# A two-layer graph network on one core: row loads moved from SyncE's queue to ScalarE's, and two units' column sums to VectorE

## Chip, core and metric

One NeuronCore of a Trainium2 chip runs the whole program. The metric is the device time of one execution in microseconds (us); lower is better.

## What is computed

`x` is 2048 x 512, `adj` is 2048 x 2048, both float32; the weight is 512 x 512. Cut to what matters:

```python
h = relu(layernorm(x))
q = round(min(h / a, 1) * 15)                      # 4-bit activations
w = round(|clip(wnorm / b, -1, 1)| * 7) * sign     # 3-bit weights
s = round(min(relu(q @ w * scale) / a2, 1) * 15)
x1 = x + adj @ s * scale                           # layer 0
h = relu(layernorm(x1))
A = (adj + adj.T) * 0.5 + I
dinv = where(rowsum(A) > 0, rowsum(A) ** -0.5, 0)
out = x1 + (1e-8 * ones) @ (dinv * A * dinv) @ h   # layer 1 of the source
```

(The last layer's coefficient matrix is in the call the adjacency itself: the function is called as `_L1_gnn(h, adj, adj)`, so the result is `x1 + adj @ ((dinv * A * dinv) @ h)`.) Both row sums and column sums of `adj` are needed for `dinv`.

## The kernel before

`adj` is worked on in 32 units: unit u is half a row block, 128 rows by 1024 columns of float32, 512 KB. Each unit has to lie in the buffer `at` transposed and split in two float16 halves ("hi", scaled by 256 and rounded, and "lo", the rest). TensorE needs them as the stationary side in layer 0 and again in the last product. A unit gets there in one of two ways:

- **Turned** units (`TURNED`): TensorE transposes the float32 unit into PSUM (`turn`, L1081), ScalarE writes hi out of PSUM (`hi_turned`, L520), VectorE writes lo (`lo_turned`, L758) and sums the columns (L745); ScalarE makes the row sum (`row_sum`, L484).
- **Moved** units (`MOVED`, 21 of them): ScalarE writes hi of the untransposed rows into a staging place (`hi_rows`, L509, which makes the row sum as well), VectorE writes lo (`lo_rows`, L763), and the SyncE queue (SP) issues two DMA transposes, hi and lo, from the staging place to `at` (`move`, L339). There are three staging places: `hi_rows` of the k-th moved unit waits until the move of the (k-3)-th has landed. The even moved units (10, 12, 14, 18, 20, 22, 26) need column sums of their own: `sum_blocks` (L496) on ScalarE, eight blocks a unit, in two calls of four. Odd moved units are added up by GpSimd into `acc` (L461, 15 additions in order), which TensorE turns once ("acc").

Layer 0 (`layer0`, L1102) has 16 rounds, one for each row block r: 32 products of 128 x 128 by 128 x 512 into one PSUM bank, with the turns of that round in between (`TURNS`). `layer0(r)` waits for `x1_ready` of round r-2, for unit 2r before its first product and for unit 2r+1 before j = 8. VectorE's `x1_tile` (L884 to L887) writes round r's result into `feat` and takes its statistics. After layer 0 come the sweeps with the symmetrized matrix (L1167, from about 159 us) and the last product (L1204, L1220).

The order on every queue is written out by hand. Per round r, VectorE does `x1_tile(r-1)`, what the turned unit needs, `lo_rows` of `MOVES[r]`, and in some rounds a late column sum (`column_sum_late`, L751: hi and lo of one unit out of `at`, in one reduction; rounds 3 and 5 for units 0 and 2) or a piece of the next stage (`sum_unit`, L930 to L935: unit 0 in round 8, unit 1 in round 10; `sum_lo`, L940). ScalarE does `hi_turned`, `hi_rows`, `row_sum` and the block sums of `SUMS_OF` in turn. SyncE does the moves, and behind them the row loads (`rows`, L314): the list `LOADS` says behind which move unit w is loaded. From unit 20 on a load overwrites an earlier unit's place, so `rows_again` first waits in `free_slot` (L318 to L329) for the readers of that unit: `acc_done` (GpSimd), `lo_ready` (VectorE), or `turned` and `rs_done`. Places for input: units 0 to 3 and 20 to 31 share the four slots of `a_in`; units 4 to 19 lie in parts of `at` that are filled later.

Turning unit 30 (round 13, L1081) waits for the lo half of unit 28 (L758); `hi_turned(28)` (L523 to L526) waits for the moves of units 26 and 27, since unit 28's place in `at` is used for staging. Before layer 0's round 14, TensorE waits for all parts of `sum_blocks`.

Of the kernel before, what the change touches and what calls it, by code (L numbers as in the profile page):

```python
# [6 lines left out]
P = 128  # L7
# [4 lines left out]
W = N // 2  # L12
B = W // P
UNITS = 2 * T
# [13 lines left out]
SUMMED = EVEN  # L28
# [6 lines left out]
def gnn_kernel(nc, x, adj, adj_scale, weight, wgt_alpha, act_alpha, act_alpha2, out):  # L35
# [5 lines left out]
    with ctx:  # L41
# [236 lines left out]
        for u in EVEN:  # L278
# [13 lines left out]
        SUMS_OF = {5: [[(10, FIRST)], [], [(10, LAST)]], 7: [[(12, FIRST)], [(12, LAST)], []],  # L292
                   8: [[(14, FIRST)], [(14, LAST)], []], 9: [[(18, FIRST)], [(18, LAST)], []],
                   10: [[], [], [(20, FIRST)]], 11: [[], [(20, LAST)], [(22, FIRST)]],
                   12: [[], [], [(22, LAST), (26, FIRST)]], 13: [[], [], [(26, LAST)]]}
        PARTS = sum(len(place) for places in SUMS_OF.values() for place in places)

# [9 lines left out]

        @block.sync
        def _(sp):
            def load_x(n):  # L310
                sp.dma_start(feat3[:, 2 * n:2 * n + 2, :], x_tiles[:, 2 * n:2 * n + 2, :]).then_inc(x_in[n], 16)

            def rows(u):
                sp.dma_start(unit_in(u), adj[(u // 2) * P:(u // 2 + 1) * P, (u % 2) * W:(u % 2 + 1) * W])\  # L314
                  .then_inc(arr_sem(u), 16)

            def rows_again(u):
                free_slot(before(u))  # L318
                rows(u)

            def free_slot(u):

                if u in ADDED:
                    sp.wait_ge(acc_done, ADDED.index(u) + 1)
                if u in MOVED:
                    sp.wait_ge(lo_ready, MOVED.index(u) + 1)
                else:
                    sp.wait_ge(turned, turn_no(u) + 1)
                    sp.wait_ge(rs_done, TURNED.index(u) + 1)  # L329

            def move(u):
                for lo, ready in ((0, hi_ready), (1, lo_ready)):
                    sp.wait_ge(ready, MOVED.index(u) + 1)
                    if u == 29:
                        wait_moved(sp, MOVED[-3])
                        wait_moved(sp, MOVED[-2])
                    elif u >= 12:
                        free_slot(waited_in(u)[lo])
                    sp.dma_start_transpose(at_half(u // 2, lo, u % 2).rearrange("p (b i) -> p b i", i=P), stage(u, lo))\  # L339
                      .then_inc(at_moved[stage_no(u)][lo], 16)  # L340
# [14 lines left out]
            rows(0)  # L355
            rows(1)
            for n in range(2, T // 2):
                load_x(n)
            for u in range(2, 12):
                rows(u)  # L360
# [3 lines left out]
            rows(12)  # L364
            rows(13)
# [3 lines left out]
            rows(14)  # L369
            rows(15)  # L370
            move(7)
            LOADS = {9: [16], 10: [17], 11: [18], 12: [19], 13: [20], 14: [21], 15: [22], 17: [23], 20: [24], 21: [25], 22: [26],
                     23: [27], 25: [29, 28], 26: [30], 27: [31]}
            for r in range(1, 12):
                for u in MOVES[r]:
                    move(u)
                    for w in LOADS.get(u, []):
                        if w < AHEAD:
                            rows(w)
                        else:  # L380
                            rows_again(w)
            for v in range(2, 6):
                free_slot(UNITS - 6 + v)
                sums(v)
# [79 lines left out]
        def _(act):  # L464
# [14 lines left out]
            def row_sum(u):  # L479
                act.wait_ge(arr_sem(u), arrivals(u))  # L480
                act.wait_ge(turned, turn_no(u) + 1)
                if u in ADDED:
                    act.wait_ge(acc_done, ADDED.index(u) + 1)
                nc.scalar.activation(unit_in(u), unit_in(u), ACT.Copy, accum_out=rowsum[:, u:u + 1]).then_inc(rs_done, 1)  # L484

# [136 lines left out]
            for r in range(1, 14):  # L622
                moves = MOVES.get(r, [])
                ahead, between, behind = SUMS_OF.get(r, [[], [], []])
                for u in TURNS[r][:1]:
                    turn_hi(u)
                for u, blocks in ahead:
                    sum_blocks(u, blocks)
                for u in moves[:1]:
                    hi_rows(u)  # L630
                for u in TURNS[r][:1]:
                    sum_rows(u)
                for u in TURNS[r][1:]:
                    turn_hi(u)
                    sum_rows(u)
                for u, blocks in between:
                    sum_blocks(u, blocks)
                for u in moves[1:]:
                    hi_rows(u)
                for u, blocks in behind:  # L640
                    sum_blocks(u, blocks)
                if r == 9:
                    sum_hi(0)
                if r == 11:
                    sum_hi(1)
# [22 lines left out]
        def _(dve):  # L668
# [278 lines left out]
            for r in range(1, 14):  # L947
# [11 lines left out]
                if r - 3 in LATE_SUMS:  # L959
                    column_sum_late(r - 3)  # L960
                if r == 8:
                    sum_unit(0)
# [8 lines left out]
            link(nc.vector.memset(pause[:, :], 0.0))  # L971
            link(nc.vector.tensor_scalar(colp[:, a:b], colp[:, a:b], 1.0 / SA, None, ALU.mult))
# [276 lines left out]
```

## Time and profile before

| | us |
|---|---|
| median of 3 runs (493.93 to 495.35) | 495.15 |
| the profiled execution's own time | 496.49 |
| its span | 494.7 |
| TensorE busy | 478.1 (97%) |
| VectorE, ScalarE, GpSimd busy | 268.5, 154.1, 46.6 |

The profile is of one execution. Its span runs from the first to the last instruction; 1.8 us of its own time lie around it. A busy TensorE is shown by modelled ends, so short idle times between matmuls read a little smaller than the distance of the starts makes them. A queue ("SPq") is an engine's sequencer: the instructions that issue DMAs stand there.

### The profile page before, as it was taken

Reading aid. Unit: us, or ns where it says so; the run is one execution under the profiler, and the core shown is the slowest. Engines: PE = TensorE matmul, PEld = TensorE weight load, DVE = VectorE, ACT = ScalarE, POOL = GpSimd, SP = SyncE. Lnnn points to the kernel's source line nnn. Section 1 sums busy time; section 2 is a strip of 40 time slices with the busy share of each in tenths; the row PEclk is TensorE's granted clock in tenths of the full one; section 3 lists DMA queues with packets and bytes.
Section 4 is the critical chain, followed back from the end, with each engine's and each line's share of the span. In section 5 each row is a group of like instructions: output and inputs, shape, how many; then the busy total and the mean of one; then the engine's idle time right before and its main releaser. Section 6 shows DMA issues by size and latency. Waiting matters only on the chain.

```text
span 494.7 us, 6414 instructions
## 1 busy us (share of the span) xinstructions
PE 478.1 (97%) x2358; PEld 232.0 (47%) x2358; DVE 268.5 (54%) x360; ACT 154.1 (31%) x300; POOL 46.6 (9%) x54
## 2 busy tenths in 40 slices
PE   1899999999999999999999999999999999999997
PEld 1755544444454444444444444444444444444446
DVE  4966996779999688876997767340100001000010
ACT  1787833767562435344521121140000000000000
POOL 2320963213200000000000000000000000000000
PEclk9999999999999999999999999999999999999999
DMA  8986999999986242332232321045010000100001
GB/s 286 401 333 161 233 193 231 225 220 229 233 241 249 65 135 98 95 117 85 85 122 91 113 99 42 0 168 193 23 42 21 21 21 21 42 21 21 21 23 43
DMA packets 63180, 62.66 MB, mean 127 GB/s; under 512 B 46136, under 2 KB 46392, under 8 KB 63160
## 3 DMA queue, kind: packets, MB, share of 16 engines
q1 hardware_dynamic: 63152, 62.40, 44.3%
q8 instruction: 11, 0.18, 0.2%
q14 instruction: 9, 0.07, 0.0%
q10 hardware_dynamic: 8, 0.00, 0.0%
HBM read 42.99 MB, written 8.39 MB: 104 GB/s over the span
## 4 chain that ended last, share of the span: by engine, by line
PE 84%; DVE 8%; DMA 4%; SPq 2%; ACT 1%; issue 1%; POOL 0%; ACTq 0%
PE ps_a L1204 31%; PE ps_p L1102 13%; PE ps_p L1167 7%; PE ps_a L1167 7%; PE ps_b L1167 7%; PE ps_m L1167 4%; PE ps_h L1167 4%; DMA feat<-in_x 2%; PE ps_b L1053 1%; PE ps_m L1102 1%; PE ps_h L1102 1%; DVE at L763 1%; DVE small L944 1%; PE ps_b L1220 1%; PE ps_a L1220 1%; PE ps_a L1053 1%
## 5 line engine op out<-in xcount | busy, mean ns | idle before, releaser
L1102 PE MATMUL ps_p<-small,at 128*128 128x512 f16 x448 | 99.2, 379 | 0.4 <-DVE feat L884 0.4
L1022 DVE SCALAR_TENSOR_TENSOR feat<-ps_a,feat 128x512 f32<-128x512 f32 (+1 forms) x16 | 10.8, 675 | 148.7 <-PE ps_a L1204 144.2
L1204 PE MATMUL ps_a<-small,at 128*128 128x512 f16 x360 | 80.2, 379 | 0.0
L1204 PE MATMUL ps_a<-a_in,at 128*128 128x512 f16 x360 | 80.2, 379 | 0.0
L1102 PEld LDWEIGHTS ps_p<-small,at 128*128 128x128 f16 x448 | 43.7, 98 | 50.8 <-DVE feat L884 0.7
L584 ACT ACTIVATE split<-a_in 128x1024 f16<-128x1024 f32 x30 | 31.7, 1057 | 101.8 <-PE ps_p L1167 90.0
L940 DVE TENSOR_TENSOR split<-a_in,split 128x1024 f16<-128x1024 f32 x30 | 36.7, 1224 | 34.0 <-ACT split L584 34.0
L1204 PEld LDWEIGHTS ps_a<-small,at 128*128 (+1 forms) x360 | 35.2, 98 | 42.5
L1204 PEld LDWEIGHTS ps_a<-a_in,at 128*128 (+1 forms) x360 | 35.2, 98 | 42.5
L1167 PE MATMUL ps_p<-feat,split 128*128 (+1 forms) x180 | 43.9, 379 | 0.5 <-DVE small L944 0.5
L1167 PE MATMUL ps_a<-feat,split 128*128 (+1 forms) x180 | 43.8, 379 | 0.0
L1167 PE MATMUL ps_b<-feat,split 128*128 (+1 forms) x180 | 43.8, 379 | 0.0
L931 DVE TENSOR_TENSOR a_in<-a_in,at 128x1024 f32<-128x1024 f32 x30 | 36.7, 1225 | 1.0
L930 DVE SCALAR_TENSOR_TENSOR a_in<-a_in,at 128x1024 f32<-128x1024 f32 x30 | 36.5, 1217 | 0.0
L1167 PEld LDWEIGHTS ps_p<-feat,split 128*128 128x128 f16 x180 | 17.5, 98 | 22.0 <-DVE small L944 1.0
L1167 PEld LDWEIGHTS ps_a<-feat,split 128*128 128x128 f16 x180 | 17.6, 98 | 21.4 <-issue 0.5
L1167 PEld LDWEIGHTS ps_b<-feat,split 128*128 128x128 f16 x180 | 17.6, 98 | 21.2
L1167 PE MATMUL ps_m<-feat,split 128*128 (+1 forms) x90 | 24.3, 379 | 0.0
L1167 PE MATMUL ps_h<-feat,split 128*128 (+1 forms) x90 | 24.3, 379 | 0.0
L461 POOL TENSOR_TENSOR at<-at 128x1024 f32<-128x1024 f32 x8 | 21.4, 2673 | 12.6 <-PE ps_p L1102 11.8
L763 DVE SCALAR_TENSOR_TENSOR at<-at 128x1024 f16<-128x1024 f32 x12 | 18.9, 1600 | 0.0
L461 POOL TENSOR_TENSOR at<-at,a_in 128x1024 f32<-128x1024 f32 x6 | 15.2, 2526 | 28.5 <-DMA a_in<-in_adj 18.4
(182 smaller groups left out, 436.0 us busy)
## 6 DMA issues: line engine op xcount, KB each, us to landing
a_in<-in_adj SPq DMA_DIRECT2D x46, 512.0 KB, 3.9
at<-in_adj SPq DMA_DIRECT2D x16, 512.0 KB, 8.9
out<-feat SPq DMA_DIRECT2D x31, 256.0 KB, 4.3
feat<-in_x SPq DMA_DIRECT2D x8, 512.0 KB, 11.6
feat<-out SPq DMA_DIRECT2D x4, 1024.0 KB, 9.3
at<-in_L_gnn_weight SPq DMA_DIRECT2D x2, 512.0 KB, 4.0
at<-at SPq DMA_TRANSPOSE x42, 4.7
split<-in_adj SPq DMA_DIRECT2D x1, 512.0 KB, 15.7
```

Of the source, the lines that this page charges most:

```text
L461: nc.gpsimd.tensor_tensor(acc, acc, unit_in(u), ALU.add).then_inc(acc_done, 1)
L584: nc.scalar.activation(part(v % 2, 0), sum_in(v), ACT.Copy).then_inc(shi, 1)
L763: nc.vector.scalar_tensor_tensor(stage(u, 1), unit_in(u), SA, stage(u, 0), ALU.mult, ALU.subtract)\
L930: link(nc.vector.scalar_tensor_tensor(u3, u3, SA, at_across(h, 0, j), ALU.mult, ALU.add))
L931: last = nc.vector.tensor_tensor(u3, u3, at_across(h, 1, j), ALU.add)
L940: nc.vector.tensor_tensor(part(v % 2, 1), sum_in(v), part(v % 2, 0), ALU.subtract).then_inc(slo, 1)
L1022: nc.vector.scalar_tensor_tensor(out, products, 1.0 / (SA * SZ), out, ALU.mult, ALU.add).then_inc(y_out, 1)
L1053: last = nc.tensor.matmul(sup_banks(m)[:, t * D:(t + 1) * D], hT[m % 2][:, (t * KD + k) * P:(t * KD + k + 1) * P], w_int[:, k * D:(k + 1) ...
L1102: last = nc.tensor.matmul(l0_bank(r), at_block(r, lo, j), small[:, j * D:(j + 1) * D], start=(j == 0 and lo == 0), stop=(j == T - 1 and lo ...
L1167: last = nc.tensor.matmul(BANK[t], part(k, lo)[:, t * P:(t + 1) * P], g_part(j, g_lo), start=(first and lo + g_lo == 0), stop=False)
L1204: last = nc.tensor.matmul(BANK[n], at_block(t, lo, j), z_part(j, z_lo), start=(j == 0 and lo + z_lo == 0), stop=(j == T - 1 and lo == 1))
L1220: last = nc.tensor.matmul(BANK[1 + h][:, 0:DH], at_block(T - 1, lo, j), z_part(j, z_lo)[:, h * DH:(h + 1) * DH], start=(j == 0 and lo + z_ ...
```

## The change

1. The loads of units 16 to 31 are issued by ScalarE, on its own DMA queue, behind `hi_rows(u)` or `sum_rows(u)` of a unit u (`load_behind`), from unit 20 on after the same `free_slot` waits, now on ScalarE. SyncE issues the moves alone in rounds 1 to 11. The list `LOADS` changes a little: unit 24 goes behind 21 instead of 20, 25 behind 22, 26 behind 23, 28 behind 24, 27 behind 25, 29 behind 26, 30 behind 27, 31 behind 29.
2. The column sums of units 10 and 14 are no longer made in `sum_blocks` on ScalarE (16 blocks less), but by `column_sum_late` on VectorE in rounds 5 and 7, and 16 sums are scaled once more behind layer 0's rounds. Units 18, 20, 22 and 26 get their block sums a round or so earlier than before, and none is left in round 13.

```diff
-SUMMED = EVEN
+SUMMED_LATE = (10, 14)
...
-        SUMS_OF = {5: [[(10, FIRST)], [], [(10, LAST)]], 7: [[(12, FIRST)], [(12, LAST)], []],
-                   8: [[(14, FIRST)], [(14, LAST)], []], 9: [[(18, FIRST)], [(18, LAST)], []],
-                   10: [[], [], [(20, FIRST)]], 11: [[], [(20, LAST)], [(22, FIRST)]],
-                   12: [[], [], [(22, LAST), (26, FIRST)]], 13: [[], [], [(26, LAST)]]}
+        SUMS_OF = {7: [[(12, FIRST)], [(12, LAST)], []], 8: [[(18, FIRST)], [(18, LAST)], []],
+                   9: [[(20, FIRST)], [(20, LAST)], []], 10: [[(22, FIRST)], [], [(22, LAST)]],
+                   12: [[], [], [(26, FIRST), (26, LAST)]]}
...
+        LOADS = {9: [16], 10: [17], 11: [18], 12: [19], 13: [20], 14: [21], 15: [22], 17: [23], 21: [24], 22: [25],
+                 23: [26], 24: [28], 25: [27], 26: [29], 27: [30], 29: [31]}
...
+        def rows(engine, u):
+            engine.dma_start(unit_in(u), adj[(u // 2) * P:(u // 2 + 1) * P, (u % 2) * W:(u % 2 + 1) * W])\
+                  .then_inc(arr_sem(u), 16)
+
+        def free_slot(engine, u):
...
         @block.sync
...
-            LOADS = {9: [16], 10: [17], 11: [18], 12: [19], 13: [20], 14: [21], 15: [22], 17: [23], 20: [24], 21: [25], 22: [26],
-                     23: [27], 25: [29, 28], 26: [30], 27: [31]}
             for r in range(1, 12):
                 for u in MOVES[r]:
                     move(u)
-                    for w in LOADS.get(u, []):
-                        if w < AHEAD:
-                            rows(w)
-                        else:
-                            rows_again(w)
...
         @block.scalar
...
+            def load_behind(u):
+                for w in LOADS.get(u, []):
+                    if w >= AHEAD:
+                        free_slot(act, before(w))
+                    rows(act, w)
...
                 for u in moves[:1]:
                     hi_rows(u)
+                    load_behind(u)
                 for u in TURNS[r][:1]:
                     sum_rows(u)
+                    load_behind(u)
...
                 for u in moves[1:]:
                     hi_rows(u)
+                    load_behind(u)
...
         @block.vector
...
                 if r - 3 in LATE_SUMS:
                     column_sum_late(r - 3)
+                for k, u in enumerate(SUMMED_LATE):
+                    if r == (5, 7)[k]:
+                        wait_moved(dve, u)
+                        column_sum_late(u)
...
             link(nc.vector.memset(pause[:, :], 0.0))
+            late_sums = colp[:, :].rearrange("p (u b) -> p u b", b=B)[:, SUMMED_LATE[0]:SUMMED_LATE[-1] + 1:4, :]
+            nc.vector.tensor_scalar(late_sums, late_sums, 1.0 / SA, None, ALU.mult)
```

## Rows read from the trace of the kernel before

**Rows 1.** Waits of TensorE, 24 to 160 us: us in total, times, longest

```profile
PE ps_a L1081 <- DVE at L758: 0.9, 1, 0.9
```

**Rows 2.** Chain that ended last, in order of time: start, us, what (rates)

```profile
139.71 0.87 PE ps_b L1081 x8
...
145.77 6.91 PE ps_h L1102 x32
```

**Rows 3.** Timeline 110 to 135 and 135 to 160 us, TensorE: start, us, instruction, [idle before <-releaser]

```profile
126.63 1.04 PE L1081 MATMUL ps_a<-ident,a_in 128*128 128x128 f32 x8
...
128.11 1.90 PE L1102 MATMUL ps_p<-small,at 128*128 128x512 f16 x8 [0.44 <-DVE feat L884]
...
136.92 1.06 PE L1081 MATMUL ps_a<-ident,a_in 128*128 128x128 f32 x8 [0.86 <-DVE at L758]
```

**Rows 4.** Timeline 110 to 135 us: VectorE, ScalarE and GpSimd

```profile
110.88 1.06 ACT L509 ACTIVATE at<-a_in 128x1024 f16<-128x1024 f32 x1 [4.16 <-DMA a_in<-in_adj]
...
112.06 2.30 DVE L763 SCALAR_TENSOR_TENSOR at<-a_in,at 128x1024 f16<-128x1024 f32 x1 [2.88 <-ACT at L509]
...
115.42 0.74 DVE L884 SCALAR_TENSOR_TENSOR feat<-ps_p,cst,feat 128x512 f32<-128x512 f32 x1
...
119.78 2.91 POOL L461 TENSOR_TENSOR at<-at,a_in 128x1024 f32<-128x1024 f32 x1 [6.49 <-DMA a_in<-in_adj]
...
120.39 3.38 DVE L930 SCALAR_TENSOR_TENSOR tmp<-tmp,at 128x1024 f32<-128x1024 f32 x1
...
127.31 0.74 DVE L884 SCALAR_TENSOR_TENSOR feat<-ps_p,cst,feat 128x512 f32<-128x512 f32 x1
...
128.91 2.33 DVE L763 SCALAR_TENSOR_TENSOR at<-a_in,at 128x1024 f16<-128x1024 f32 x2
...
133.37 1.02 ACT L520 ACTIVATE at<-ps_a 128x1024 f16<-128x1024 f32 x1 [4.88 <-DMA at<-at]
```

**Rows 5.** Timeline of SyncE's queue, 100 to 107.2 and 119 to 134.5 us

```profile
99.26 2.65 SPq L339 DMA_TRANSPOSE at<-at  x2
101.96 0.58 SPq L314 DMA_DIRECT2D a_in<-in_adj  x1
...
106.51 0.53 SPq L314 DMA_DIRECT2D a_in<-in_adj  x1
...
119.60 1.88 SPq L314 DMA_DIRECT2D a_in<-in_adj  x2
```

**Rows 6.** ScalarE's block sums L496 and VectorE's late sums L751

```profile
L496 ACT ACTIVATE ps_h<-at x4: 364/367/368, 71.9 to 76.8; 128x256 f32<-128x256 f16 x4
...
L751 DVE TENSOR_REDUCE colp<-at x2: 2272/2272/2272, 68.3 to 80.2; 128x8 f32<-128x2048 f16 x2
```

**Rows 7.** Row loads L314: issued 57 to 132 us, and the two of 119.9 to 122

```profile
L314 SPq DMA_DIRECT2D a_in<-in_adj x12: 521/532/1253, 77.9 to 131.5; - x12
...
DMA to landing us min/median/max: 4.2/4.6/5.9
...
DMA to landing us min/median/max: 4.8/5.2/5.6
```

**Rows 8.** The page's groups: busy us, mean ns of one, idle before

```profile
L930 DVE SCALAR_TENSOR_TENSOR a_in<-a_in,at 128x1024 f32<-128x1024 f32 x30 | 36.5, 1217 | 0.0
```

**Rows 9.** Moves issued 92 to 102.5, then 102.5 to 120 us: time to landing

```profile
DMA to landing us min/median/max: 3.1/3.3/5.4
...
DMA to landing us min/median/max: 4.2/5.0/6.1
```

**Rows 10.** Stretches: us; busy PE, PEld, DVE, ACT, POOL; clock, DMA share, GB/s

```profile
92.00:102.00 10.00, 10.00 (x48) 4.51 (x46) 7.59 (x9) 6.94 (x26) 4.24 (x2) 1.00 1.02 202
102.00:120.00 18.00, 18.00 (x89) 8.70 (x88) 14.40 (x16) 11.89 (x37) 2.58 (x2) 1.00 1.09 234
```

**Rows 11.** Timeline of VectorE, 144 to 145 and 156 to 161 us

```profile
144.45 0.18 DVE L972 TENSOR_SCALAR colp<-colp 128x24 f32<-128x24 f32 x1
...
159.62 0.75 DVE L884 SCALAR_TENSOR_TENSOR feat<-ps_m,cst,feat 128x512 f32<-128x512 f32 x1 [0.75 <-PE ps_m L1102]
```

More of the change, by code:

```diff
@@ L306, in arrivals @@
             return 16 if u < AHEAD else 16 * ((u - AHEAD) // RING + 2)
+        def rows(engine, u):
+            engine.dma_start(unit_in(u), adj[(u // 2) * P:(u // 2 + 1) * P, (u % 2) * W:(u % 2 + 1) * W])\
+                  .then_inc(arr_sem(u), 16)
+        def free_slot(engine, u):
+            if u in ADDED:
+                engine.wait_ge(acc_done, ADDED.index(u) + 1)
+            if u in MOVED:
+                engine.wait_ge(lo_ready, MOVED.index(u) + 1)
+            else:
+                engine.wait_ge(turned, turn_no(u) + 1)
+                engine.wait_ge(rs_done, TURNED.index(u) + 1)
         @block.sync
@@ L311, in load_x @@
                 sp.dma_start(feat3[:, 2 * n:2 * n + 2, :], x_tiles[:, 2 * n:2 * n + 2, :]).then_inc(x_in[n], 16)
[L313 to L326, printed above, removed]
-                else:
-                    sp.wait_ge(turned, turn_no(u) + 1)
-                    sp.wait_ge(rs_done, TURNED.index(u) + 1)
             def move(u):
@@ L337, in move @@
                     elif u >= 12:
-                        free_slot(waited_in(u)[lo])
+                        free_slot(sp, waited_in(u)[lo])
                     sp.dma_start_transpose(at_half(u // 2, lo, u % 2).rearrange("p (b i) -> p b i", i=P), stage(u, lo))\
@@ L354, in _ @@
                 load_x(n)
-            rows(0)
-            rows(1)
+            rows(sp, 0)
+            rows(sp, 1)
             for n in range(2, T // 2):
@@ L359, in _ @@
             for u in range(2, 12):
-                rows(u)
+                rows(sp, u)
             sums(0)
@@ L363, in _ @@
             sp.wait_ge(hT_ps, T // 2)
-            rows(12)
-            rows(13)
+            rows(sp, 12)
+            rows(sp, 13)
             move(3)
@@ L368, in _ @@
             sp.wait_ge(sq_ready, T // 2)
-            rows(14)
-            rows(15)
+            rows(sp, 14)
+            rows(sp, 15)
             move(7)
-            LOADS = {9: [16], 10: [17], 11: [18], 12: [19], 13: [20], 14: [21], 15: [22], 17: [23], 20: [24], 21: [25], 22: [26],
-                     23: [27], 25: [29, 28], 26: [30], 27: [31]}
             for r in range(1, 12):
@@ L376, in _ @@
                     move(u)
-                    for w in LOADS.get(u, []):
-                        if w < AHEAD:
-                            rows(w)
-                        else:
-                            rows_again(w)
             for v in range(2, 6):
-                free_slot(UNITS - 6 + v)
+                free_slot(sp, UNITS - 6 + v)
                 sums(v)
```

## Prediction

> **What bounds the kernel now.** I read the table first: TensorE is busy 97% of the span, so the question is where the rest is and whether this change reaches it. The waits of TensorE between 24 and 160 us, where the change works, leave little: the longest is 0.9 us before a turn, for VectorE's L758 [rows 1]. The timeline places them. The turn of unit 28 starts at 126.63 and has 8 matmuls; a turn takes 0.87 us [rows 2], so it ends at 127.50, and the products of round 12 start at 128.11, after VectorE's `x1_tile(10)` [rows 3]: 0.61 us lost. Round 12 has 32 products at 6.91 us and the turn "acc" of 0.87 [rows 2], so from 128.11 it ends at 135.89; unit 30's turn starts at 136.92 [rows 3]: 1.03 us lost. Together **1.64 us**. Everywhere else in this stretch the starts of the matmuls follow each other without a hole, so this is the most that the change can bring in layer 0.
>
> Who is late? Going back from 136.92: VectorE's lo of unit 28, ScalarE's hi of it at 133.37 after 4.88 us of idling for a DMA transpose [rows 4], the lo move of unit 27. That move could only be issued once `lo_rows(27)` was through, the first of the two at 128.91 [rows 4]. `lo_rows(27)` stood behind `x1_tile(10)` at 127.31, this behind `sum_unit(1)` from 120.39, this behind `x1_tile(9)` at 115.42, and the head of this unbroken VectorE chain is `lo_rows(25)` at 112.06, which had waited 2.88 us for ScalarE, and ScalarE 4.16 us for unit 25 to arrive [rows 4]. Both holes of TensorE thus come from one late load: unit 25 was asked for at 106.51, behind unit 21's moves [rows 5].
>
> **Loads to ScalarE.** On SyncE's queue a load and two transposes took 4.55 us (101.96 to 106.51), two transposes without a load 2.65 [rows 5]. Of the loads, unit 25's counts. Now ScalarE issues it behind `hi_rows(22)`, once `lo_rows(21)` is done. That was done before unit 21's second transpose went out, and the first went out right behind the load at 101.96, so some time between 102 and 104. The late sum of unit 14 may push it 2.27 us on [rows 6], at most. So the load goes out between 102 and 104.5 (with ends this near I take 103.5), and with 4.2 to 5.9 us to landing [rows 7] it is there at about 108.3 instead of 110.9. `lo_rows(25)` starts at about 109.5 instead of 112.06, and TensorE's round 9 ends at 126.63 - 2 x 6.91 - 0.87 = 111.94, so `x1_tile(9)` starts at about 112.5 instead of 115.42: **the chain is 2 to 3 us earlier**.
>
> Behind it may lie more. `sum_unit(1)`'s first step took 3.38 us [rows 4] where the mean is 1.22 [rows 8], beside GpSimd's addition of unit 27 at 119.78, which itself had waited 6.49 us for its load [rows 4]. With units 27 and 29 loaded earlier, these additions come before or behind `sum_unit(1)`: zero to 2 us more. I take 3 us for `x1_tile(10)`: 124.3 instead of 127.31. The first hole needs 0.61 and is gone. `lo_rows(27)` comes as much earlier. Its move had 3.1 us to landing; beside a load such moves had a median of 5.0 [rows 9], and unit 31's load now goes out at the same moment, since both wait for `lo_rows(27)`. So of 3 us some 1.9 may be given back: hi of unit 28 starts 1.1 to 3 us earlier, or more by GpSimd's part. The second hole needs 1.64 (its own 1.03 and the 0.61 by which TensorE now comes earlier). I take the hole as closed, since 1.1 is the corner and not the middle, and keep 0 to 0.5 us left over for the range.
>
> **What ScalarE pays.** 16 loads at 0.53 us [rows 7] are 8.5 us; 16 block sums less, at 0.37 us and the reading of each sum, about 0.4, are 6.4 us. Net 2 us over some 80 us in which it is busy about two thirds (11.89 of 18 us [rows 10]); idling covers it. What it pays in order is more delicate: its waits in `free_slot` now hold everything behind them, `hi_rows` and `hi_turned` among them. Followed for the tightest: the turn of unit 24 ends at 126.63 - 2 x 6.91 = 112.8 as before; then hi of it (1.02), four block sums of unit 22 (1.6), `hi_rows(26)` (1.15), load 29 (0.55), the row sum (1.15), so load 28 goes out at about 118.4, lands by 122.6 to 124.3, and is needed at 126.63. Before, it was the second of the two loads from 119.60 [rows 5], at most 5.6 us to landing [rows 7], and there some 0.8 us ahead of its turn.
>
> **What SyncE gains.** Its moves no longer stand behind loads and their waits. Nothing that TensorE waits for hangs on it but units 26 and 27 above. The loads of the next stage wait on `rs_done` of units 28 to 31 as before and come with the turns.
>
> **Late sums on VectorE.** Two at 2.27 us [rows 6]. Unit 10's, in round 5, and unit 14's, in round 7, lie before the head of the chain; VectorE idled 10 - 7.59 = 2.4 us between 92 and 102 and 3.6 us between 102 and 120 [rows 10], and the second of these covers what the first doesn't. `x1_tile` has a round (6.91) of slack. Both moves have long landed. If that cover were gone, a sum costs up to 2.27 us of the chain's 3. The new scaling of 16 sums is like the one of 24, 0.18 us, in a chain that ends before VectorE idles 0.75 us for TensorE [rows 11]: nothing. No block sum is left in round 13, so round 14 doesn't wait for one now that TensorE comes earlier.
>
> **Sum.** -0.61 - 1.03 = -1.64 us; costs 0. The profiled execution's 496.49 becomes 494.85. It stands 1.34 above the median, so against that: 495.15 - 1.64 = **493.5**. Behind layer 0 everything keeps its distance to TensorE and shifts with it.
>
> **A rule that speaks against it.** Between 92 and 102 us, with a single load, the engines' share of busy time is 1.02, and 1.09 with loads between 102 and 120 [rows 10]: they look full either way. The Trainium skill (DMA: Bandwidth & Descriptors, "Issuing engines are not separate DMA queues") says that DMAs of different issuing engines run on the same 16 DMA engines and interleave, so only the issue time is saved. By it the transposes would lose what the loads win, and the time would come out at about 494.5. The sum above doesn't rest on more bandwidth, but on asking for unit 25 earlier.
>
> **Rivals.**
> 1. *The engines are the limit (0.17).* For it: the shares just named, and 4.55 against 2.65 us, which is a load's time whichever queue it is in. Unit 25 still comes earlier, but each move lands 1.9 us later, the first hole closes and the second stays: 495.15 - 0.61 = 494.5.
> 2. *VectorE is no earlier (0.08).* The late sum of unit 14 moves `lo_rows(21)`, `lo_rows(23)` and with them the `free_slot` waits of loads 25 and 27, so that they go out when they did. Against it: it takes 2.27, the load wins 2 to 4.5. No change, 495.15.
> 3. *ScalarE is blocked and unit 28 comes late (0.07); slower.* Place: the turn of unit 28 at 126.63. Each us by which its load lands later costs one; since both holes are then swallowed, it decides from 126.63 + 1.64 = 128.3, that is 4 to 5.7 us later than worked out. Each of loads 25 to 29 waits on ScalarE for VectorE or GpSimd, and such waits add up through `hi_rows` and its transposes, which themselves delay `lo_rows`. At 6 to 8 us of such delay unit 28 is there at about 130.3: +2.0, 497.2.
> 4. *The loads stay tied to the old order (0.03):* ScalarE, in order, reaches them no sooner than SyncE did. 495.15.
>
> **Numbers.** The forecast, both holes closed, has 0.65; 0.17, 0.08, 0.07 and 0.03 for the rivals. About 0.3% (1.5 us) is what a measurement of this kernel can tell from no change. The forecast's 1.64 lies just over it; the runs shown differ by 1.4, so a median may stray by some 0.5, and I give it 0.72 to be seen as faster, 0.28 as the same. Faster: 0.65 x 0.72 + 0.17 x 0.1 = 0.48, with the rest 0.01 for a chain that I missed: 0.49. Slower: 0.06. Same: 0.45. Range: 492.5 (1.64, the stray of a median and the 0.5 by which two medians differ) to 495.8 (rivals 1, 2, 4 and the stray); rival 3 is left out.
>
> **What would show it.** Right: the load of unit 25 issued by ScalarE before 104.5 and `lo_rows(25)` before 110.5; `x1_tile(10)` before 126; no idle time before the products of round 12, nor before the turn of unit 30; round 14 in the chain at 144.1 rather than 145.77 [rows 2]; SyncE's moves pairwise in about 2.7 us. Rival 1: moves landing 5 us and more after issue while loads run, a hole before unit 30's turn. Rival 3: TensorE idle before unit 28's turn for a DMA. The prediction is wrong if TensorE has a new wait anywhere between 50 and 126 us, or if the sweeps no longer follow without a hole.

## The result, and the profile after

The changed kernel takes **508.48 us** (median of 6 runs, 500.19 to 515.92), the kernel before 495.24 beside it (493.93 to 495.35). The ratio is 1.0164, 95% interval 1.0128 to 1.0199: slower, where 493.5 was forecast. The ratios in this text compare only runs within 1.5% of a kernel's fastest (here 500.19, 502.64 and 506.61), so they can be smaller than the quotient of the medians. The profiled execution is one of the longer ones: 513.68 us, span 511.8, against 496.49 and 494.7. The sizes read from it below are therefore those of a long execution; a shorter one of nearly the same kernel, 508.82 us, follows among the experiments and shows the same kinds of waits.

The waits of TensorE in the whole span, of after (the waits for `scal_row` and `wstat` lie outside layer 0 and were there before):

```profile
PE ps_p L1109 <- DMA at<-at: 6.0, 2, 4.9
...
PE ps_a L1088 <- DMA a_in<-in_adj: 5.4, 1, 5.4
...
PE ps_a L1088 <- DVE at L759: 2.1, 1, 2.1
```

Where there had been one wait of 0.9 us [rows 1] there are now four, three of them for DMAs. The timeline of TensorE places them (layer 0's products are L1109 now, turns L1088):

```profile
82.94 1.04 PE L1088 MATMUL ps_a<-ident,at 128*128 128x128 f32 x8
85.10 7.07 PE L1109 MATMUL ps_p<-small,at 128*128 128x512 f16 x32 [1.12 <-DMA at<-at]
97.08 23.18 PE L1109 MATMUL ps_p<-small,at 128*128 128x512 f16 x96 [4.91 <-DMA at<-at]
120.09 1.04 PE L1088 MATMUL ps_b<-ident,a_in 128*128 128x128 f32 x8
120.96 13.98 PE L1109 MATMUL ps_p<-small,at 128*128 128x512 f16 x64
140.33 1.97 PE L1088 MATMUL ps_a<-ident,a_in 128*128 128x128 f32 x8 [5.39 <-DMA a_in<-in_adj]
142.09 3.62 PE L1109 MATMUL ps_p<-small,at 128*128 128x512 f16 x8
145.50 1.35 PE L1088 MATMUL ps_b<-ident,at 128*128 128x128 f32 x8
146.69 5.34 PE L1109 MATMUL ps_p<-small,at 128*128 128x512 f16 x24
154.08 1.06 PE L1088 MATMUL ps_a<-ident,a_in 128*128 128x128 f32 x8 [2.06 <-DVE at L759]
```

With 0.216 us a product and 0.87 a turn [rows 2], the distances of the starts give the holes: 1.29 before 85.10, 5.07 before 97.08 (11.98 less 32 products), 5.55 before 140.33 (19.37 less 64 products), 2.21 before 154.08: **14.12 us**. The two holes before 97.08 and 140.33 cost a second time. Behind 97.08 the 96 products take 23.01 us instead of 20.74; behind 140.33 the turn takes 1.76 instead of 0.87, the 8 products 3.41 instead of 1.73, the turn "acc" 1.19 instead of 0.87: 5.16 us in all. The stretches (us; busy PE, PEld, DVE, ACT, POOL; granted clock, DMA share, GB/s) show why, and something else:

```profile
68.00:72.00 4.00, 4.00 (x20) 1.83 (x19) 3.58 (x4) 0.00 (x0) 2.35 (x1) 1.00 0.80 70
...
92.00:96.00 4.00, 0.17 (x1) 0.00 (x0) 3.93 (x6) 0.00 (x0) 2.34 (x1) 0.87 1.24 95
96.00:100.00 4.00, 2.92 (x7) 1.04 (x8) 2.61 (x3) 2.95 (x11) 0.00 (x0) 0.50 1.10 211
...
140.00:144.00 4.00, 3.67 (x13) 2.46 (x14) 2.01 (x4) 0.00 (x0) 0.00 (x0) 0.50 1.50 124
```

After TensorE had idled some 5 us, its granted clock is 0.50, which is the level of 1.2 GHz. So 14.12 - 1.64 (the holes of before) + 5.16 = 17.6 us; the spans differ by 17.1, and TensorE had started layer 0's turns 0.5 us earlier than before. The loss of this execution is accounted for.

The other thing is in the last two columns: at 68 to 72 us the DMA engines moved 70 GB/s, at 92 to 96 us 95 GB/s, with a busy share of 0.80 and 1.24. The kernel before moved 202 GB/s between 92 and 102 us [rows 10], and at 68 to 72 us, from its trace:

```profile
68.00:72.00 4.00, 4.00 (x20) 1.77 (x19) 3.93 (x5) 1.16 (x3) 2.07 (x1) 1.00 0.87 201
```

So the DMA engines are about as busy as before, or more so, and move a third to a half of the data. The transfers show it. ScalarE's loads (L312) issued between 56 and 150 us, the one issued at 62.24 alone, then the moves (L338) issued in 56 to 150, and those issued at 132 to 134 us alone:

```profile
DMA to landing us min/median/max: 4.4/6.5/11.8
...
DMA to landing us min/median/max: 11.2/11.2/11.2
...
DMA to landing us min/median/max: 3.2/7.3/16.0
...
DMA to landing us min/median/max: 12.4/14.2/16.0
```

Before, loads took 4.2 to 5.9 [rows 7], moves at most 6.1 [rows 9]. Not every load is slow. In the order of issue, start and time to landing of ScalarE's loads are, from the trace:

```text
55.6+4.6  60.7+4.9  62.2+11.2  73.6+4.4  75.4+9.4  85.2+4.6  86.7+10.2  105.3+4.5
110.2+4.6  112.2+9.3  121.8+4.5  124.9+6.5  128.5+11.8  130.2+11.4  137.8+11.8
```

In this trace a load that goes out while ScalarE's previous one has not landed, with moves in flight, takes 9 to 12 us (once 6.5); one that goes out with no other load of ScalarE's in flight takes 4.4 to 4.9. Moves in flight with a slow load are stretched too: the slowest beside each took 10.4 to 16.0 us. ScalarE then waits for staging places: the wait of `hi_rows` (L507) for moves grew from 13.3 us in 5 to

```profile
  DMA at<-at: 37.8, 9
```

and the chain between 60 and 160 us is no longer TensorE's. Its shares by line were 44.5% for layer 0's products in `ps_p` and 3.1% for `DMA at<-at`; now:

```profile
by line: DMA at<-at 55.3%; SPq L338 14.5%; DVE at L764 9.7%; issue 5.1%; PE ps_p L1109 4.1%; ACT at L507 3.6%; DVE feat L885 2.0%; DVE st L887 1.7%; ACT ps_m L494 1.6%; ACT ps_h L494 1.4%; DVE split L932 1.2%; DVE colp L746 1.2%; DVE split 
```

### The profile page after: what moved, and what is told of

Read it like the earlier page. It is cut to its first block, busy times and chain, and to the rows that moved or that the text cites. A ratio compares the mean times of both kernels' runs of the same rounds, so it can differ in the third digit from the quotient of the medians.

```text
span 511.8 us, 6383 instructions
## 1 busy us (share of the span) xinstructions
PE 484.4 (95%) x2358; PEld 234.8 (46%) x2358; DVE 270.4 (53%) x363; ACT 147.8 (29%) x268; POOL 46.5 (9%) x54
## 3 DMA queue, kind: packets, MB, share of 16 engines
q10 hardware_dynamic: 2312, 8.39, 7.9%
HBM read 42.99 MB, written 8.39 MB: 100 GB/s over the span
## 4 chain that ended last, share of the span: by engine, by line
PE 70%; DMA 13%; DVE 8%; SPq 4%; ACT 3%; issue 2%; POOL 0%; ACTq 0%
PE ps_a L1211 30%; DMA at<-at 11%; PE ps_p L1174 7%; PE ps_a L1174 7%; PE ps_b L1174 7%; PE ps_m L1174 4%; PE ps_h L1174 4%; SPq L338 3%; DVE at L764 2%; DMA feat<-in_x 2%; PE ps_p L1109 2%; PE ps_b L1060 1%; PE ps_m L1109 1%; PE ps_h L1109 1%; DVE small L945 1%
## 5 line engine op out<-in xcount | busy, mean ns | idle before, releaser
L1109 PE MATMUL ps_p<-small,at 128*128 128x512 f16 x448 | 103.3, 390 | 6.0 <-DMA at<-at 6.0
L1109 PEld LDWEIGHTS ps_p<-small,at 128*128 128x128 f16 x448 | 44.6, 100 | 59.3 <-issue 11.4
L1174 PEld LDWEIGHTS ps_a<-feat,split 128*128 128x128 f16 x180 | 17.6, 98 | 21.4 <-issue 0.5
L1174 PEld LDWEIGHTS ps_b<-feat,split 128*128 128x128 f16 x180 | 17.6, 98 | 21.2
L764 DVE SCALAR_TENSOR_TENSOR at<-at 128x1024 f16<-128x1024 f32 x12 | 19.0, 1594 | 10.4 <-ACT at L507 10.4
L453 POOL TENSOR_TENSOR at<-at 128x1024 f32<-128x1024 f32 x8 | 21.3, 2667 | 12.6 <-PE ps_p L1109 11.8
L507 ACT ACTIVATE at<-at 128x1024 f16<-128x1024 f32 x12 | 12.6, 1052 | 29.7 <-DMA at<-at 29.7
```

What stands on the lines that cost most here:

```text
L453: nc.gpsimd.tensor_tensor(acc, acc, unit_in(u), ALU.add).then_inc(acc_done, 1)
L507: nc.scalar.activation(stage(u, 0), unit_in(u), ACT.Copy, scale=SA, accum_out=rowsum[:, u:u + 1])\
L764: nc.vector.scalar_tensor_tensor(stage(u, 1), unit_in(u), SA, stage(u, 0), ALU.mult, ALU.subtract)\
L1109: last = nc.tensor.matmul(l0_bank(r), at_block(r, lo, j), small[:, j * D:(j + 1) * D], start=(j == 0 and lo == 0), stop=(j == T - 1 and lo ...
L1174: last = nc.tensor.matmul(BANK[t], part(k, lo)[:, t * P:(t + 1) * P], g_part(j, g_lo), start=(first and lo + g_lo == 0), stop=False)
```

## The experiments

Two theories stand in what follows. Theory A: row loads and DMA transposes that run beside each other from two queues slow each other, whatever their order. Theory E, formed when the third kernel missed: what is slow is a second load of ScalarE's queue, issued while its first is in flight beside transposes. Other explanations stand as rivals in the expectations.

**Each half alone.** The first kernel is the kernel before with the second part of the change (`SUMMED_LATE`, the new `SUMS_OF`, the late sums and their scaling), the second is the changed kernel without it.

```diff
-SUMMED = EVEN
+SUMMED_LATE = (10, 14)
```

> The second half of the change alone: the column sums of units 10 and 14 late on VectorE and the new list of block sums; all loads stay on SyncE's queue in their old order. Theory A (row loads on one queue and DMA transposes on another hinder each other in the 16 DMA engines): no loss, 494 to 496. Rival B (the late sums and the new order of ScalarE's work hold up hi_rows and lo_rows, and the moves with them): most of the loss is here, 500 to 508.

494.7 us (10 runs, 494.03 to 495.85), ratio 1.0003 [0.9989, 1.0016]. Both old holes are still there, in its timeline of TensorE:

```profile
127.47 1.90 PE L1107 MATMUL ps_p<-small,at 128*128 128x512 f16 x8 [0.66 <-DVE feat L883]
...
136.29 1.06 PE L1086 MATMUL ps_a<-ident,a_in 128*128 128x128 f32 x8 [0.87 <-DVE at L757]
```

> The first half alone: the loads of units 16 to 31 issued by ScalarE, sums as before. Theory A: the whole loss, 500 to 512, with TensorE waiting for moves or loads that take 9 us and more to land. Rival B: 494 to 497.

506.78 us (504.06 to 513.79), ratio 1.0198 [1.0177, 1.0219], in theory A's range. In the profiled execution (508.82 us) TensorE waits 8.1 us for moves, and the load at 60.6 us takes 12.6 to land. The loads alone make the loss; by themselves the late sums do nothing. Overlap is not always as dear, though: a load that went out here 2.1 us behind the one before, at 113.4 us, landed in 6.3.

**SyncE's moves wait for the loads.** In the changed kernel, `move(u)` first waits until the loads behind unit u have landed.

```diff
+                for w in LOADS.get(u, []):
+                    sp.wait_ge(arr_sem(w), arrivals(w))
```

> The changed kernel, but SyncE holds the moves of a unit back until the load that ScalarE issued behind the same unit has landed, so that loads and transposes overlap much less; every other queue and order is as in the changed kernel. Theory A: most of the loss comes back, 495 to 500, and loads land in under 6 us. Rival C (ScalarE is blocked in free_slot and everything behind it is late): more waiting only adds, 508 to 520.

510.22 us (508.53 to 512.75), ratio 1.0326 [1.0294, 1.0358]: theory A missed, and the number lies in rival C's range. The wait doesn't part what I meant it to. Moves already in flight stay beside the loads, and ScalarE issues its second load meanwhile: 60.1 and 61.7 us, 74.2 and 75.9, 86.7 and 88.3. The first of each pair lands in 4.4 to 4.5 us, the second in 12.1, 10.7 and 10.6. The pair, not the mixture, is what the slow ones have in common. It isn't enough by itself: five later loads of this execution, from 112 to 131 us, also went out with one of ScalarE's still in flight and landed in 4.5 to 6.3 us.

**Transfers alone, in long runs.** A kernel of nothing but transfers:

```diff
+            for k in range(TR):
+                sp.dma_start_transpose(dst(k), src(k)).then_inc(tr_in[k], 16)
...
+            for k in range(LD):
+                act.dma_start(rows_act[:, k * W:(k + 1) * W], adj_rows(k)).then_inc(act_in[k], 16)
```

> The two kinds of transfer by themselves, in six phases one after the other; nothing of the network is computed, the output is x. Phases: 12 transposes on SyncE (as many and as large as 6 moved units); 6 row loads on SyncE; both on SyncE, a load and two transposes in turn; both at once, transposes on SyncE and loads on ScalarE; 6 loads on each queue; transposes on SyncE and loads on ScalarE, one load in flight at a time. From the traces: 16 us, 8 to 12, and 27 (6 x 4.55) for the first three. Theory A: the fourth and sixth take 35 us or more, while the fifth, without transposes, takes 16 to 20. Rival D (the engines only share their time between the queues): the fourth takes as long as the third or less, 20 to 28.

The same 12 transposes and 6 loads, on one queue in turn and on two:

```profile
33.05:61.14 28.09, 0.00 (x0) 0.00 (x0) 1.00 1.04 224
61.59:87.66 26.07, 0.00 (x0) 0.00 (x0) 1.00 0.98 241
```

The expected loss isn't there: two queues are 2 us faster. Theory A, that mixing alone is slow, falls. Single transfers are stretched here as well, a load to 10.0 us and a transpose to 12.1, but the total isn't. With one load in flight at a time (the sixth phase) the same transfers take 27.6 us, so where nothing collapses that wait costs a little.

**One load of ScalarE in flight.** The changed kernel, where ScalarE waits for its previous load before it issues the next:

```diff
+            loaded = []
...
                 for w in LOADS.get(u, []):
+                    if loaded:
+                        act.wait_ge(arr_sem(loaded[-1]), arrivals(loaded[-1]))
+                    loaded.append(w)
```

> The changed kernel, but ScalarE issues no load before its previous one has landed. Theory E (what is slow is a second load queued on ScalarE's queue while transposes are on SyncE's; a lone load beside transposes landed in 4.4 to 4.9 us in the changed kernel, a second one in 9 to 12): loads land in under 6 us, 495 to 500, though ScalarE waits more. Theory A in its plain form (any overlap of load and transposes is slow in this kernel): 503 to 515. Rival C (blocked ScalarE): also over 503, but with loads that land fast.

**494.19 us** (10 runs, 493.06 to 495.26), ratio 0.9977 [0.9966, 0.9988], the fastest kernel of this study and a little below theory E's range of 495 to 500. ScalarE waits for loads in addition and the kernel is faster, so blocking ScalarE (rival C) isn't what made the loss. Its loads and moves issued between 56 and 150 us land in:

```profile
DMA to landing us min/median/max: 4.0/4.4/6.5
...
DMA to landing us min/median/max: 3.2/5.0/7.9
```

and TensorE between 112 and 140 us:

```profile
112.99 13.98 PE L1114 MATMUL ps_p<-small,at 128*128 128x512 f16 x64
126.80 1.04 PE L1093 MATMUL ps_a<-ident,a_in 128*128 128x128 f32 x8
127.67 1.89 PE L1114 MATMUL ps_p<-small,at 128*128 128x512 f16 x8
...
130.27 5.34 PE L1114 MATMUL ps_p<-small,at 128*128 128x512 f16 x24
135.70 1.06 PE L1093 MATMUL ps_a<-ident,a_in 128*128 128x128 f32 x8
```

Round 12 follows its turn at once, unit 30's turn comes 0.25 us behind the products where it had been 1.03 [rows 3].

**The same transfers in the network kernel's places, beside busy engines.** Transfers beside work that computes nothing of the network:

```diff
+            for k in range(12):
+                sp.dma_start_transpose(dst(k), src(k)).then_inc(tr_in[k], 16)
+            done(sp, 4)
```

> The transfers by themselves once more, now in the network kernel's own places in SBUF; the network is not computed, the output is x. Six phases: both queues at once (12 transposes on SyncE, 6 loads on ScalarE) with idle engines; three groups of 4 transposes beside 2 loads 1.2 us apart, idle engines; both queues at once beside TensorE's matmuls; the same beside VectorE and GpSimd at work; the same beside all three; one queue in turn beside all three. The earlier run of the same transfers in other places took 26 us on two queues and 28 us on one, so mixing alone isn't slow. If the places matter, the first phase takes 35 us or more; if two queued loads do, the second does (over 12 us a group); if an engine's accesses matter, the phase beside it. If all take 24 to 30, something else of the kernel is needed.

Two queues beside TensorE, beside VectorE and GpSimd, beside all three, and one queue beside all three:

```profile
79.87:107.50 27.63, 27.27 (x120) 12.07 (x120) 0.00 (x0) 0.00 (x0) 0.00 (x0) 1.00 1.04 228
107.95:134.28 26.33, 0.00 (x0) 0.00 (x0) 25.82 (x8) 0.00 (x0) 25.47 (x9) 0.55 0.97 240
134.73:161.56 26.83, 26.51 (x116) 11.77 (x117) 26.55 (x9) 0.00 (x0) 26.11 (x9) 0.94 1.00 235
162.00:190.59 28.59, 26.50 (x123) 11.86 (x121) 28.18 (x10) 0.00 (x0) 27.79 (x10) 1.00 1.03 221
```

Busy engines make it no slower than idle ones did (30.4 us in this kernel, where the first transpose took 15 us to land, 26.07 in the one before), so they are no part of it. Of three short groups (four transposes, two loads) one took 12.35 us, with a second load of 8.6; the order in time seemed to matter, which was an impression and not yet shown.

**An earlier load on one queue.** The kernel before, where loads 24 to 27 and 29 to 31 go out between a unit's hi and lo move:

```diff
+                    if lo:
+                        for w in EARLY.get(u, []):
+                            rows_again(w)
```

> The kernel before, all on SyncE's queue, with the loads of units 24 to 27 and 29 to 31 one step earlier: between the hi and the lo move of the unit behind which they stood (28 stays). The prediction's own reasoning without a second queue: unit 25 arrives some 2.6 us earlier, VectorE's chain starts earlier, both holes of TensorE close, -1.6 us, 493.2. Rival: the moves are pushed back as far as the loads win, no change.

498.59 us (497.06 to 498.92), ratio 1.0062 [1.0042, 1.0081]: missed by both, and slower. The first hole is closed (0.06 us left), the second has grown to 2.75. The lo moves go out behind a load and its waits, and unit 30's turn waits longer, with a half-speed turn behind it:

```profile
137.47 1.79 PE L1086 MATMUL ps_a<-ident,a_in 128*128 128x128 f32 x8 [2.59 <-DVE at L763]
```

**Groups of transfers.** Kind f of the kernel, on ScalarE (`spend(1)` is one activation of 1.06 us):

```diff
+                if kind == "f":
+                    spend(3)
+                    load_f(0)
+                    spend(1)
+                    load_f(1)
```

> Transfers alone, 30 groups with nothing else at work; of the network nothing is computed and the output is x. Each group holds 4 transposes of a move's size on SyncE's queue (6 in kind f), and both queues wait for all of it before the next group. Kinds, 5 of each: a) one load on ScalarE's queue; b) two loads some 1.3 us apart; c) two loads back to back; d) the second load only when the first has landed; e) everything on SyncE's queue, load, two transposes, load, two transposes; f) two loads 1.3 us apart, begun some 4 us behind the first of six transposes. Theory E (a second load in flight on ScalarE's queue beside transposes is what stretches all that is in flight): a load lands in 4 to 5 us in a, d and e, the second load takes 8 to 12 us in b, c and f, and groups b and c are 2 us or more longer than e. Rival (the slow loads need something else of the network kernel, since transfers alone did not show them so far): the second load of b, c and f stays below 7 us and b, c are within 1 us of e.

The five groups of each kind, a to f in order (us; busy DVE, ACT, POOL; clock, DMA share, GB/s):

```profile
11.56:55.56 44.00, 0.00 (x0) 0.00 (x0) 0.00 (x0) 1.00 0.85 179
55.56:107.73 52.17, 0.00 (x0) 6.56 (x6) 0.00 (x0) 1.00 0.92 201
107.73:159.25 51.52, 0.00 (x0) 0.00 (x0) 0.00 (x0) 1.00 0.91 204
159.25:212.34 53.09, 0.00 (x0) 0.00 (x0) 0.00 (x0) 1.00 0.90 198
212.34:265.44 53.10, 0.00 (x0) 0.00 (x0) 0.00 (x0) 1.00 0.90 198
265.44:356.03 90.59, 0.00 (x0) 21.12 (x20) 0.00 (x0) 1.00 1.01 145
```

b and c miss theory E's numbers: as long as e, second loads of 4.8 to 8.8 and 5.5 to 7.0 us. f meets them, every time: second loads of 9.3 to 12.8 us, transposes up to 13.7, at 145 GB/s. So two loads beside transposes are not enough. In f there are six transposes, and the first load comes in when the third of them has been issued and two are in flight; in the changed kernel, too, two or three moves were in flight when each slow load went out. Which of the two differences from b, the later start or the larger number, counts is not parted here.

**Dose and share.** The kernel with one load in flight, first with the column sums as before (the second half of the change undone), then with the wait for the loads up to unit 23 alone:

```diff
-                    if loaded:
+                    if loaded and w < 24:
```

> The loads on ScalarE's queue with one in flight at a time, and the column sums of units 10 and 14 on ScalarE as in the kernel before. If the late column sums have no share in the gain of the changed kernel with one load in flight (494.19), this gives 494.0 to 494.4, as the kernel with the sums alone (ratio 1.0003) suggests. If ScalarE's 16 more block sums delay hi_rows or the loads behind them, 494.7 to 496.

497.9 us (11 runs, 495.64 to 499.21), ratio 1.0053 [1.0034, 1.0072]: missed, and slower than before. Its loads are quick (3.9 to 5.7 us). But ScalarE, which now waits for loads, still has units 22 and 26's sums to make in rounds 12 and 13, and `split` (L588) comes late for VectorE, last at 131.67 us after a wait of 3.22, ahead of the work that unit 30's turn waits for. ScalarE's and VectorE's waits in 94 to 140 us:

```profile
ACT ps_h L500 <- DMA a_in<-in_adj: 8.4, 4, 3.2
...
DVE split L947 <- ACT split L588: 5.8, 2, 3.2
```

```profile
136.89 1.91 PE L1088 MATMUL ps_a<-ident,a_in 128*128 128x128 f32 x8 [2.65 <-DVE at L765]
```

Unit 30's turn comes late and, behind 2.65 us of idle, takes 1.70 us by the starts instead of 0.87. Worth nothing alone, the second half of the change (the late sums together with the new list of block sums, which this run undoes as one) is worth 3.7 us here (497.9 against 494.19).

> The changed kernel where only the loads up to unit 23 wait for ScalarE's previous load; those of 24 to 31 go out as in the changed kernel. Theory E: TensorE's waits before 100 us (1.3 and 5.2 us in the changed kernel) are gone, the one of some 5.7 us before unit 30's turn is still there with a stretch at half clock behind it, and the time is 498 to 506. If the late waits are only a consequence of the early ones (the order of the work shifted by them), they go too: 494 to 495.

498.37 us (10 runs, 494.34 to 512.85), ratio 1.0047 [1.002, 1.0074], just inside theory E's range. The early waits are gone. (The text above says "unit 30's turn" for the wait of some 5.7 us; by the order of the turns it is unit 28's.) The profiled execution is a short one, 495.62: its late loads overlap and take up to 8.0 us, unit 28's 7.1, and TensorE waits 0.3 for it and 1.0 before unit 30's turn. There is no collapse in it, though six of its late loads went out with another of ScalarE's in flight and with two or three moves. The times spread from 494.34 to 499.76 in eight runs, with 506.05 and 512.85 in the other two, where the kernel with all loads in turn spreads over 2.2 us. That the late waits are the reason for the spread is likely but not shown, since none of the long executions was profiled.

**Six transposes, and what comes on top.**

```diff
+                    if kind == "k" and k >= 2:
+                        sp.wait_ge(tr_in[k - 2], 16 * t[k - 2])
+                    if kind == "l" and k in (2, 3):
+                        load(k - 2)
```

> Transfers alone again, 30 groups of six transposes of a move's size on SyncE's queue, nothing of the network computed, the output is x; both queues wait for a whole group before the next. 5 groups of each kind, one after the other: g) six transposes alone; h) one load on ScalarE's queue 3.4 us behind the first transpose; i) two loads from there, the second issued when the first has landed; j) two loads 1.5 us apart, as in kind f of the groups before (14.7 to 19.9 us a group there); k) as j, but SyncE issues a transpose only when the last but one has landed, so that two are in flight; l) everything on SyncE's queue, the loads behind the second and the third transpose. Theory E (two loads of ScalarE's queue in flight beside a queue of transposes are what collapses): g takes 8 to 9.5 us, h 10 to 11.5, i and l 12.5 to 14, j 15 to 20 as before, and the slow loads (over 8 us) are in j alone. Rival (any load that comes in while five transposes are queued collapses, whether alone or not): h and i are slow too, 12 us or more for h and 16 or more for i, with loads over 8 us. Kind k tells whether the depth of the transposes' queue has a part: 12.5 to 14.5 us with loads under 7 us if it has, 15 or more if the two loads do it by themselves.

Kinds g to l, five groups each:

```profile
11.57:62.03 50.46, 0.00 (x0) 0.00 (x0) 0.00 (x0) 1.00 0.82 156
62.03:125.07 63.04, 0.00 (x0) 17.12 (x16) 0.00 (x0) 1.00 0.93 167
125.07:195.84 70.77, 0.00 (x0) 15.84 (x15) 0.00 (x0) 1.00 0.91 185
195.84:288.06 92.22, 0.00 (x0) 21.12 (x20) 0.00 (x0) 1.00 1.01 142
288.06:384.44 96.38, 0.00 (x0) 21.12 (x20) 0.00 (x0) 1.00 0.93 136
384.44:450.69 66.25, 0.00 (x0) 0.00 (x0) 0.00 (x0) 1.00 0.91 198
```

ScalarE's loads in i, then in j, and SyncE's in l:

```profile
DMA to landing us min/median/max: 4.2/4.8/6.0
...
DMA to landing us min/median/max: 5.4/9.7/12.3
...
DMA to landing us min/median/max: 4.4/5.1/6.2
```

A fifth of each stretch is a group: 10.1 us for transposes alone, 12.6 with one load, 14.2 with two in turn, **18.4** with two in flight, 13.3 on one queue. The same bytes take 4 us longer when the second load doesn't wait for the first. That is theory E's order, not all of its numbers: g is above its 9.5 us, h above its 11.5 and i just above its 14. One load alone is a little slow too (5.4 to 6.7 us) and h reaches the rival's 12, but i stays below the rival's 16, and no load of h or i is over 8 us. In j every second load takes 11.3 to 12.3 us. Kind k was the surprise: only two transposes in flight, and 19.3 us, with second loads of 10.4 to 11.4. So a long row of transposes in flight isn't needed; ScalarE's second load is. How much of k's 19.3 us is its own waiting stays open, as it has no group without loads, and in j no more than four transposes are in flight either: issuing one took up to 7.3 us there, 1.3 in g.

**The new list, one queue.** The changed kernel with all loads back behind the moves on SyncE:

```diff
-                    load_behind(u)
...
                     move(u)
+                    for w in LOADS.get(u, []):
+                        if w >= AHEAD:
+                            free_slot(sp, before(w))
+                        rows(sp, w)
```

> The changed kernel with its new list of loads and its late column sums, but all loads back on SyncE's queue behind the moves (unit 28 behind 25, since 24 is not moved). It tells the queue from the list. Theory E (the collapse needs loads on a second queue): no load takes over 8 us and TensorE runs at full clock, but unit 24 to 27 now stand one move later than in the kernel before (a move is some 4 us apart there), so that the waits before round 12 and unit 30's turn grow from 1.6 us to 3 to 6: 496 to 500. If the new list alone made the changed kernel slow, 503 to 510 with loads of 9 to 12 us. If the list and the late sums alone give what the kernel with one load in flight gives, 494.2.

501.09 us (500.06 to 501.24), ratio 1.0113 [1.0086, 1.014], one us above the range of theory E. No load is slow (4.0 to 6.5 us), not even the second of two issued 0.4 us apart, but GpSimd gets unit 29 at 130.8 us, and the turn "acc" waits for it:

```profile
PE ps_b L1083 <- POOL at L457: 5.6, 1, 5.6
```

That TensorE would run at full clock did not hold: behind this wait the turn and the 24 products took 8.39 us by the starts instead of 6.05. So the list is made for the second queue, and the slow loads are the second queue's, not the list's.

## Why the prediction was wrong

**What held.** The two holes and their cause. With the collapse taken away, unit 25's load goes out at 102.2 us (I took 103.5) and lands at 106.6 (108.3), `lo_rows(25)` starts at 110.63 (109.5; `hi_rows(25)` stood behind four block sums and a staging place), `x1_tile(10)` at 123.86 (124.3), and both holes close but for 0.25 us. The gain is 0.93 us of the 1.64 worked out (494.19 against 495.12 for the kernel before beside it; the ratio gives 1.14). That is the prediction's mechanism, but in a kernel that has a wait which the prediction did not have. The late sums alone and the scaling cost nothing, as costed.

**The step that failed** is in "What ScalarE pays" and "Sum": "costs 0". The change was costed as 16 issues on ScalarE and as earlier transfers, each with the landing times of before: 4.2 to 5.9 us for a load, 1.9 more for a move beside one. On SyncE's queue those times held: a load mostly stood behind two transposes, some 4.5 us behind the load before, and the one pair of loads that went out together, from 119.60 us, landed in 4.8 and 5.6 [rows 7]. On ScalarE's own queue nothing spaces them: after a stall the waits in `free_slot` and for staging places are over together and two loads go out some 1.5 to 3.5 us apart, on top of running moves. Then, in that trace, a load lands in 9 to 12 us (once in 6.5) and a move in up to 16. In the six profiled network kernels whose loads ScalarE issued, no load issued after 50 us with none of ScalarE's in flight took over 6.5 us; with one in flight they took 4.5 to 12.6. So the overlap is needed for the loss and does not always bring it. The term was 0 and measured 17.6 us in the profiled execution, 12.5 of idling and 5.16 of TensorE at half clock behind it; over the runs that the ratio compares the kernel lost 1.6%, some 8 us. And it feeds itself: late moves hold `hi_rows` (37.8 us), and when they land, two `hi_rows` and two loads follow at once. The trace had no row loads or moves on a second queue, so nothing in it priced this; the bound I put on it, a move's 1.9 us, came from a single queue and was no bound for two.

**Rival 1** (the engines are the limit, 494.5) had the right quantity, the landing of moves, and not its size: moves issued between 56 and 150 us landed in 7.3 us at the median and 16.0 at most, where they had taken 4.7 and 6.1, against the rival's 1.9 more for each. The rule of the Trainium skill (DMA: Bandwidth & Descriptors, "Issuing engines are not separate DMA queues") that DMAs of different engines interleave on the same 16 engines agrees with long runs, where two queues took 26.07 us and one 28.09; in kind j against l of the groups they don't just interleave, the same bytes take 18.4 us against 13.3.

**Rival 3** (ScalarE blocked, unit 28 late, 0.07) had sign and place: the largest hole lies before unit 28's turn, since its load went out at 128.5 instead of the 118.4 worked out and took 11.8 us. Its mechanism was only half of it: ScalarE was blocked mostly by moves, not by `free_slot`, and the rival's price was 2.0 us. That its sign came out is partly luck. **Rivals 2 and 4** are answered by the kernel with one load in flight: unit 25's load goes out at 102.2 us, not at 106.51, with the late sum in place and ScalarE in order. Rival 2's opposite turned up instead: the second half of the change is needed once ScalarE waits for loads (3.7 us).

**The sign of being wrong** that the prediction named was a new wait of TensorE between 50 and 126 us; there are two, before 85.10 and before 97.08. The range left out rival 3, the only one that ended above it.

**What stays open.** Why a second load on another queue slows everything when transposes have been running, and doesn't in a long run begun together (26.07 us) or, mostly, in groups of four. Nor is it known why some overlapping loads land in 4.5 to 6.3 us (the later ones of the kernel whose moves wait) and others in 9 to 12. In the slow stretches the DMA engines' busy share stays near 1 (0.80 to 1.24) at 70 to 145 GB/s, so a packet takes longer on average; what holds them the runs don't show. Loads alone on two queues, six on each, took 19.9 us at 316 GB/s, so without transposes nothing collapsed; whether it takes transposes or any transfers of small packets wasn't tried, nor a queue of a third engine.

## What to carry to other kernels

Moving DMAs to a second queue takes away more than their issue time from the first: it takes away the spacing that the order of one queue gave them. Before doing it, ask what then spaces them, and try bounding them to one in flight if DMA transposes run beside them; here that wait made 508.48 into 494.19. It isn't free: without the second half of the change it ended at 497.9, and in the long row of transfers it cost 1.6 us (27.6 against 26.07). A landing time read in a trace holds for the queues and the order it was read in, and an experiment on transfers must copy the order in time, not only the kinds and bytes.

## What the runs showed of the hardware

Two 512 KB loads, 1.5 us apart on one queue, begun 3.4 us behind the first of six DMA transposes on another, take 18.4 us together with them, against 13.3 on one queue and 14.2 with the second load held back, at 142 GB/s with a DMA busy share of 1.01; holding the transposes to two in flight doesn't help (19.3). Busy TensorE, VectorE and GpSimd make mixed transfers no slower (26.3 to 27.6 us for the same work, 26.07 and 30.4 with idle engines).

Issuing a transpose took SyncE 1.23 to 1.35 us in the row of six alone, but up to 7.45 us in the changed kernel between 56 and 150 us (3.34 at most in the kernel before). The issues over 5 us stand among the slow landings there, so the queue that issues is held up as well. And a load cost ScalarE 0.33 to 0.37 us to issue in the changed kernel, where SyncE's took 0.53 [rows 7]. That is not the engine alone: SyncE's first load behind a pause took 0.33 in the long rows of transfers, and six in a row on ScalarE took 3.31, 0.55 each.
